# Moving DMA issues among a displaced convolution's engine queues

## The chip, the core and the metric

The kernel runs on one core of a Trainium2 chip. Its time is the device time of one execution in microseconds (us), and a comparison uses the median over several runs. The engines are PE (TensorE: matrix products, with PEld its weight loads), DVE (VectorE), ACT (ScalarE), POOL (GpSimd) and SP (SyncE). A DMA is issued by an instruction in the queue of one engine (here SP and ACT) and carried out by 16 shared DMA engines.

## The reference

Input x has shape (32, 384, 64, 64) in float32, with 48 offsets of two numbers. Each image is normalised in groups of 12 channels, each group of 8 channels is shifted by its rounded offset (zeros come in from outside), a 5 x 5 Gaussian of the offset's fraction is applied per channel, and the input is added.

```
def _gn(v, G=32, eps=1e-5):            # 12 channels a group
    g = v.reshape(B_, G, C_ // G, H_, W_)
    return ((g - mean(g)) / sqrt(var(g) + eps)).reshape(v.shape)

def _L0_conv_ref(x, offset):           # offset: (48, 2)
    off_round = round(offset)
    disp = _displace(x.reshape(B, 48, 8, h, w), off_round)
    d = field[None] + (offset - off_round)[:, None, None, :]
    kernel = exp(-sum(d * d, -1) / (2.0 * SIGMA ** 2))
    kernel = kernel / sum(kernel, axis=(1, 2))
    return depthwise_conv5x5(disp, repeat(kernel, 8))

out = x + _L0_conv_ref(_gn(x), offset)
```

## The kernel before

Shift and filter are separable, so each channel's plane is multiplied from both sides by small matrices: `ay` for the rows (the y products, line 750) and `ax` for the columns (the x products, line 762). The 384 channels are taken in 16 superblocks `c` of 24 channels, and each superblock in 16 steps `s` of two images (`B = 2`); `t` counts steps over the whole kernel. One step's input is a slot `xin[:, s]` of SBUF, 16 slots in all; the result is added in place in the slot and stored from there. A step's load is two DMAs on SP, one for each image (line 199), and its store is two DMAs on ACT (line 674). SP loads slot s for the next superblock when the slot's store has landed (`stored[s]`).

Steps are worked in rounds of four (`QUAD`), four rounds a superblock, 64 rounds in all. Each engine runs its own hand-written order and they meet through semaphores. In the order of one round on PE: the x products of its steps, `x_products(0)` to `x_products(3)`, 96 matmuls each; then y products of the next round's steps (`y_even`, `y_odd`, 96 matmuls each), with the statistics' sums (line 737, 8 matmuls) behind the first and the third. `x_products(0)` waits for `sums_ready`; `x_products(1)` waits for all four copies of the y results (`y_ready`, `last_lane_ready`); `x_products(2)` waits for copy_third of step t and DVE's addition of step t, and `x_products(3)` for those of step t+1.

ACT's round, in order, is: store 0 of the last round, `copy_y(t)` (PSUM to `y`, line 651), `normalise(t+2)` (line 640), `copy_y(t+1)`, store 1, `normalise(t+3)`, `copy_y(t+2)`, stores 2 and 3, `copy_y(t+3)`, `copy_third(t)` and `copy_third(t+1)` (line 668, PSUM to `x2`), `normalise(t+4)`, `copy_third(t+2)`, `normalise(t+5)`, `copy_third(t+3)`. What stands behind a DMA issue in this order starts once the issue is through. DVE computes the statistics of coming steps (line 502, three a step, running 17 ahead), copies one lane of y (526), reduces the sums (518) and adds two thirds of the result (533); POOL turns sums into coefficients, normalises the other half (341) and adds the last third (332).

At the start SP loads slots 0 to 11 at once and 12 to 15 behind a wait on `x_done`, which reaches 4 when `x_products(1)` of the first round is done. `y_done` counts y products, the first, third and so on only together with the sums behind them; it reaches 5 when the y product and the sums behind the first round's x products are done. At the end ACT issues the last round's four stores and then raises `norm0_ready` (line 724), for which PE's last pass, one pair of y products that no output reads, waits. SP ends when all stores have landed (line 211).

Of the kernel before, what the change touches and what calls it, by code (L numbers as in the profile page):

```python
# [11 lines left out]
P = 128  # L12
POSITIONS = 48
B = 2
# [4 lines left out]
NSUPER = CH // SUPER  # L19
# [10 lines left out]
STEPS = BATCH // B  # L30
TOTAL = NSUPER * STEPS
SLOTS = 16
PAIR = 2
QUAD = 4
# [11 lines left out]
def displaced_conv(nc: bass.Bass, x: bass.AP, offset: bass.AP, out: bass.AP):  # L46

    def tiled(a):
        return a.rearrange("(m b) (s q a) (h r) w -> m b s (a h) q (r w)", b=B, s=NSUPER, q=Q, a=LANES, r=R)

    x_t, out_t = tiled(x), tiled(out)
    off_row = offset.rearrange("(o p) k -> o (p k)", o=1)

    with ExitStack() as ctx:
        def sb(name, shape, dt=F32):
            return ctx.enter_context(nc.sbuf_tensor(name, shape, dt))

        def sem(name):
            return ctx.enter_context(nc.semaphore(name))


        xin = sb("xin", [P, SLOTS, Q, ROW])
# [69 lines left out]
        stored = [sem(f"stored{i}") for i in range(SLOTS)]  # L132
# [15 lines left out]
        y_done = sem("y_done")  # L148
# [3 lines left out]
        x_done = sem("x_done")  # L152
        x2_ready = sem("x2_ready")
        result0_ready = sem("result0_ready")
        result1_ready = sem("result1_ready")
# [20 lines left out]
        ADDS = 2  # L176
        SPARE = 2
# [3 lines left out]
        def run(one_round):  # L181

            def superblock(c, head=False, tail=False):
                for g in range(ROUNDS):
                    one_round(c, g, head and g == 0, tail and g == ROUNDS - 1)
            superblock(0, head=True)
            with nc_engine[0].Fori(1, NSUPER - 1) as c:
                superblock(c)
            superblock(NSUPER - 1, tail=True)
# [3 lines left out]
        @block.sync  # L193
        def _(sync):
            sync.dma_start(off[:, :, :], off_row.to_broadcast([P, 2 * POSITIONS])).then_inc(off_loaded, 16)

            def load(c, s):
                for b in range(B):
                    sync.dma_start(xin[b:P:B, s], x_t[s, b, c]).then_inc(loaded[s], 16)

            for s in range(SLOTS):
                if s == FIRST:

                    sync.wait_ge(x_done, ADDS * PAIR)
                load(0, s)
            with sync.Fori(1, NSUPER) as c:
                for s in range(SLOTS):
                    sync.wait_ge(stored[s], 16 * B * c)
                    load(c, s)
            for s in range(SLOTS):  # L210
                sync.wait_ge(stored[s], 16 * B * NSUPER)

# [384 lines left out]
        def _(act):  # L597
# [15 lines left out]
            def square(c, part):  # L613
                source, target = ((t_int, t_isq), (t_full, t_fsq))[part]
                act.wait_ge(dist_ready, 2 * c + part + 1)
                nc.scalar.activation(target[:], source[:], ACT.Square).then_inc(sq_ready, 1)

            def exponential(c):
                act.wait_ge(sq_ready, 2 * c + 2)
                nc.scalar.activation(t_exp[:], t_fsq[:], ACT.Exp, scale=-2.0).then_inc(exp_ready, 1)  # L620

            def fill_rows(c, k):

                act.wait_ge(made, c + 1)
                if k == 0:

                    act.wait_ge(half0_ready, STEPS * (c + 1))
                for part in range(1 - k, B):
                    filled_k = nc.scalar.activation(ay[:, k].rearrange("p r (m b) -> p (r m) b", b=B)[:, :, part],  # L629
                                                    t_msk[:, k, 0:R].rearrange("p r m -> p (r m)"), ACT.Identity,  # L630
                                                    scale=same[:, part:part + 1])
                filled_k.then_inc(mats_ready[k], STEPS)

            def normalise(t, s, quad, first=False):
                act.wait_ge(coef_ready, (s // PAIR + 1) if first else quad + 2)
                if not (first and s < 2):
                    act.wait_ge(y_done, t - 1)
                cv, col = s // QUAD % 2, GROUPS * (s % QUAD)
                cols = slice(0, QG * HW)
                nc.scalar.activation(norm[:, s % 2, :, cols].rearrange("p r (q w) -> p q r w", w=HW),  # L640
                                     xin[:, s, 0:QG].rearrange("p q (r w) -> p q r w", w=HW),
                                     ACT.Identity, bias=bias[:, cv, col:col + 1],
                                     scale=rstd[:, cv, col:col + 1]).then_inc(norm0_ready, 1)

            def copy_y(t, j, first):

                lanes = LANES if j == 2 else LANES - 1
                act.wait_ge(y_done, t + 1)
                if not first:
                    act.wait_ge(x_done, ADDS * (t - QUAD + 1))  # L650
                nc.scalar.activation(y[:, j].rearrange("p k r a m -> p a (k r) m")[:, 0:lanes],  # L651
                                     ps[:, j % 2, 0:lanes, 0:POS * P].rearrange("p a (n m) -> p a n m", m=32),
                                     ACT.Copy).then_inc(y_ready, 1)
# [10 lines left out]
            def copy_third(t, s, first=False):  # L664
                act.wait_ge(x_done, ADDS * (t + 1))
                if not first:
                    act.wait_ge(result0_ready, t - QUAD + 1)
                nc.scalar.activation(x2[:, s % QUAD], ps[:, s % 2, 2:4, 0:ROW], ACT.Copy).then_inc(x2_ready, 1)  # L668

            def store(c, s, t):  # L670
                act.wait_ge(result0_ready, t + 1)
                act.wait_ge(result1_ready, SPARE + t + 1)
                for b in range(B):
                    act.dma_start(out_t[s, b, c], xin[b:P:B, s]).then_inc(stored[s], 16)

            def one_round(c, g, first, last):
                t, s, quad = STEPS * c + QUAD * g, QUAD * g, ROUNDS * c + g
                group_follows = c is not NSUPER - 1

                def store_of_last_round(j):  # L680
                    if not first:
                        store(c if g else c - 1, (s - QUAD + j) % STEPS, t - QUAD + j)

                if group_follows:
                    if g == 1:
                        square(c + 1, 0)
                    if g == 2:
                        square(c + 1, 1)
                    if g == 3:
                        exponential(c + 1)  # L690
                store_of_last_round(0)
                copy_y(t, 0, first)
                act.wait_ge(last_lane_ready, t + 1)
                normalise(t + 2, s + 2, quad, first)
                copy_y(t + 1, 1, first)
                store_of_last_round(1)
                act.wait_ge(last_lane_ready, t + 2)
                normalise(t + 3, s + 3, quad, first)
                copy_y(t + 2, 2, first)
                store_of_last_round(2)  # L700
                store_of_last_round(3)
                copy_y(t + 3, 3, first)
                border = g == ROUNDS - 1 and group_follows
                if border:
                    fill_rows(c + 1, 0)
                copy_third(t, s, first)
                copy_third(t + 1, s + 1, first)
                if not last:
                    normalise(t + 4, (s + 4) % STEPS, quad + 1)
                copy_third(t + 2, s + 2, first)  # L710
                if border:
                    fill_rows(c + 1, 1)
                if last:
                    store(c, s, t)
                else:
                    normalise(t + 5, (s + 5) % STEPS, quad + 1)
                copy_third(t + 3, s + 3, first)
                if last:
                    for j in range(1, QUAD):
                        store(c, s + j, t + j)  # L720
            run(one_round)

            act.wait_ge(norm0_ready, TOTAL)
# [151 lines left out]
```

## Time and profile before

| | us |
|---|---|
| median of 3 runs | 1249.34 (1246.99 to 1251.42) |
| profiled execution, its own time | 1246.37 |
| its span, first to last instruction | 1244.5 |
| PE busy | 1155.9 (93%) |
| DVE busy | 968.7 (78%) |
| POOL busy | 853.0 (69%) |
| ACT busy | 750.7 (60%) |
| DMA, mean over the span | 324 GB/s, 402.99 MB |

The span is the trace's, and the execution's own time has 1.9 us more around it. Busy time of an engine leaves out the instructions that issue DMAs: ACT's 60% does not hold the time for which its queue is taken by them. In a timeline ACTq and SPq are these issues.

### The profile page before, as it was taken

The numbers are of one execution on the slowest core, as the hardware profiler recorded it, in microseconds if no ns is written. First come the engines' busy times: TensorE is split into PE (matmuls) and PEld (weight loads), VectorE is DVE, ScalarE is ACT, GpSimd is POOL, SyncE is SP. The second block draws the span as 40 slices with busy tenths as digits, with TensorE's granted clock in tenths as the row PEclk, the third lists the DMA queues.
The fourth block names the chain that finished last, engine by engine and source line by source line (L and its number), as shares of the span: only waits on it lengthen the run. The fifth ranks groups of instructions, "written<-read, shape, count | busy, mean of one in ns | idle before, by whom it ended". The sixth has DMA issues, their size and how long they took to land. (4 is left out here: it accounts for less than half of the span.)

```text
span 1244.5 us, 113105 instructions
## 1 busy us (share of the span) xinstructions
PE 1155.9 (93%) x50608; PEld 1130.8 (91%) x50608; DVE 968.7 (78%) x1373; ACT 750.7 (60%) x874; POOL 853.0 (69%) x1176
## 2 busy tenths in 40 slices
PE   7799999999999999999999999999999999999997
PEld 7799999989989999999889999999999999999997
DVE  8578878877877878878778878878778788878762
ACT  4465665655656665665666666666666666656562
POOL 7477676676776766766776766866766776766763
PEclk9899999999999999999999999999999999999998
DMA  9599999999999999999999999999999999999966
GB/s 305 182 326 332 330 344 343 326 342 329 334 337 330 330 344 329 336 341 327 335 325 321 350 343 326 343 347 325 344 334 317 349 322 347 340 345 330 343 201 202
DMA packets 409763, 402.99 MB, mean 324 GB/s; under 512 B 16528, under 2 KB 409744, under 8 KB 409744
## 3 DMA queue, kind: packets, MB, share of 16 engines
q10 hardware_dynamic: 204800, 201.36, 48.9%
q1 hardware_dynamic: 204944, 201.41, 48.9%
q8 instruction: 8, 0.13, 0.1%
q14 instruction: 11, 0.09, 0.0%
HBM read 201.38 MB, written 201.33 MB: 324 GB/s over the span
## 5 line engine op out<-in xcount | busy, mean ns | idle before, releaser
L750 PE MATMUL ps<-ay,norm 32*128 32x128 f32 x24768 | 749.4, 274 | 10.0 <-ACTq L724 6.6
L750 PEld LDWEIGHTS ps<-ay,norm 32*128 32x128 f32 x24768 | 716.9, 188 | 22.1 <-issue 8.9
L651 ACT ACTIVATE y<-ps 128x1152 f32<-128x1152 f32 (+1 forms) x256 | 310.1, 1211 | 349.5 <-PE ps L762 156.9
L502 DVE BATCH_NORM_STATS2 stats<-xin 128x6 f32<-128x512 f32 x768 | 482.5, 693 | 0.0
L762 PEld LDWEIGHTS ps<-ax,y 64*64 64x64 f32 x24576 | 379.2, 135 | 84.6 <-issue 77.0
L762 PE MATMUL ps<-ax,y 64*64 64x64 f32 x24576 | 388.3, 219 | 72.2 <-issue 69.0
L533 DVE TENSOR_TENSOR xin<-ps,xin 128x1024 f32<-128x1024 f32 x256 | 313.6, 1225 | 145.4 <-PE ps L762 145.2
L341 POOL TENSOR_SCALAR norm<-xin,rstd,bias 128x768 f32<-128x768 f32 x256 | 251.9, 987 | 126.1 <-issue 105.9
L332 POOL TENSOR_TENSOR xin<-x,xin 128x512 f32<-128x512 f32 x256 | 322.5, 1281 | 7.7 <-ACT x L668 7.5
L640 ACT ACTIVATE norm<-xin,bias,rstd 128x768 f32<-128x768 f32 x256 | 261.3, 1021 | 35.3 <-issue 34.9
L668 ACT ACTIVATE x<-ps 128x512 f32<-128x512 f32 x256 | 151.3, 591 | 86.0 <-PE ps L762 85.9
L314 POOL TENSOR_TENSOR mean_sq<-both 128x8 f32<-128x8 f32 (+1 forms) x65 | 50.9, 784 | 207.9 <-DVE both L518 205.9
L526 DVE COPY y<-ps 128x384 f32<-128x384 f32 x192 | 106.2, 553 | 65.1 <-PE ps L737 40.6
L324 POOL TENSOR_TENSOR rstd<-var,mhalf 128x8 f32<-128x8 f32 (+1 forms) x65 | 105.8, 1627 | 5.1
L518 DVE TENSOR_REDUCE both<-ps 128x24 f32<-128x288 f32 x63 | 28.8, 458 | 48.1 <-ACT y L651 48.1
L737 PE MATMUL ps<-summands,ones 32*128 32x72 f32 (+1 forms) x1040 | 47.8, 250 | 1.0 <-POOL summands L295 1.0
L737 PEld LDWEIGHTS ps<-summands,ones 32*128 32x128 f32 x1040 | 42.9, 190 | 1.5 <-issue 0.9
L629 ACT ACTIVATE ay<-t_msk,same 128x256 f32<-128x256 f32 x48 | 23.4, 525 | 2.4 <-DVE ay L495 2.4
L295 POOL TENSOR_TENSOR summands<-stats 128x24 f32<-128x24 f32 (+1 forms) x65 | 15.0, 230 | 9.8 <-POOL summands L293 9.7
L487 DVE SCALAR_TENSOR_TENSOR t_msk<-t_isq,t_exp 128x960 f32<-128x960 f32 x16 | 18.4, 1149 | 0.0
L321 POOL TENSOR_TENSOR var<-spread,mean_sq 128x8 f32<-128x8 f32 (+1 forms) x65 | 14.0, 215 | 5.2 <-POOL spread L319 0.2
L319 POOL TENSOR_TENSOR spread<-inner,both 128x8 f32<-128x8 f32 (+1 forms) x65 | 13.8, 213 | 5.4
(63 smaller groups left out, 215.2 us busy)
## 6 DMA issues: line engine op xcount, KB each, us to landing
xin<-in_x_dram SPq DMA_DIRECT2D x512, 384.0 KB, 5.8
out_dram<-xin ACTq DMA_DIRECT2D x512, 384.0 KB, 5.1
off<-in_L_conv_offset_dram SPq DMA_DIRECT2D x1, 48.0 KB, 3.6
```

Source lines behind the costliest of these rows:

```text
L324: pool.tensor_tensor(rstd[:, v, part], var[:, v, part], mhalf[:, part], ALU.pow).then_inc(small, 1)
L332: pool.tensor_tensor(at, x2[:, s % QUAD], at, ALU.add).then_inc(result0_ready, 1)
L341: pool.tensor_scalar(norm[:, s % 2, :, cols].rearrange("p r (q w) -> p q r w", w=HW), xin[:, s, QG:].rearrange("p q (r w) -> p q r w", w=H ...
L502: nc.vector.bn_stats(stats[:, s // QUAD % 2, s % QUAD, n, :], xin[:, s].rearrange("p (g q) f -> p q f g", g=GROUPS)[:, n]).then_inc(bn_don ...
L526: nc.vector.tensor_copy(y[:, j].rearrange("p k r a m -> p a (k r) m")[:, LANES - 1], ps[:, j % 2, LANES - 1, 0:POS * P].rearrange("p (n m) ...
L533: nc.vector.tensor_tensor(at, ps[:, s % 2, 0:2].rearrange("p h (k f) -> p h k f", k=2), at, ALU.add).then_inc(result1_ready, 1)
L640: nc.scalar.activation(norm[:, s % 2, :, cols].rearrange("p r (q w) -> p q r w", w=HW), xin[:, s, 0:QG].rearrange("p q (r w) -> p q r w", ...
L651: nc.scalar.activation(y[:, j].rearrange("p k r a m -> p a (k r) m")[:, 0:lanes], ps[:, j % 2, 0:lanes, 0:POS * P].rearrange("p a (n m) -> ...
L668: nc.scalar.activation(x2[:, s % QUAD], ps[:, s % 2, 2:4, 0:ROW], ACT.Copy).then_inc(x2_ready, 1)
L737: last = nc.tensor.matmul(ps[:, v, a, place], ones[rows, :], summands[rows, part].rearrange("p t n s -> p (t n s)"), start=True, stop=True)
L750: last = nc.tensor.matmul(ps[:, v, a, P * k:P * (k + 1)], norm[rows, v, r, P * k:P * (k + 1)], ay[rows, k, r, :], start=(r == 0), stop=(r ...
L762: last = nc.tensor.matmul(ps[outs, v, 2 * (k // 2) + h, at:at + HW], y[rows, j, k, r].rearrange("p a m -> p (a m)")[:, outs], ax[rows, k], ...
```

## The change

Four edits. SP's loads of slots 12 to 15 in the first superblock wait for `y_done` 5 instead of `x_done` 4. In each round ACT issues store 1 behind `normalise(t+3)` instead of ahead of it, and store 3 behind `copy_y(t+3)` instead of ahead of it. In the last round ACT issues each store's first image alone, and SP issues the second image, waiting for the same two semaphores.

```diff
--- before.py
+++ after.py
@@ -201,12 +201,17 @@
             for s in range(SLOTS):
                 if s == FIRST:
 
-                    sync.wait_ge(x_done, ADDS * PAIR)
+                    sync.wait_ge(y_done, QUAD + 1)
                 load(0, s)
             with sync.Fori(1, NSUPER) as c:
                 for s in range(SLOTS):
                     sync.wait_ge(stored[s], 16 * B * c)
                     load(c, s)
+
+            for s in range(STEPS - QUAD, STEPS):
+                sync.wait_ge(result0_ready, TOTAL - STEPS + s + 1)
+                sync.wait_ge(result1_ready, SPARE + TOTAL - STEPS + s + 1)
+                sync.dma_start(out_t[s, 1, NSUPER - 1], xin[1:P:B, s]).then_inc(stored[s], 16)
             for s in range(SLOTS):
                 sync.wait_ge(stored[s], 16 * B * NSUPER)
 
@@ -667,10 +672,10 @@
                     act.wait_ge(result0_ready, t - QUAD + 1)
                 nc.scalar.activation(x2[:, s % QUAD], ps[:, s % 2, 2:4, 0:ROW], ACT.Copy).then_inc(x2_ready, 1)
 
-            def store(c, s, t):
+            def store(c, s, t, images=B):
                 act.wait_ge(result0_ready, t + 1)
                 act.wait_ge(result1_ready, SPARE + t + 1)
-                for b in range(B):
+                for b in range(images):
                     act.dma_start(out_t[s, b, c], xin[b:P:B, s]).then_inc(stored[s], 16)
 
             def one_round(c, g, first, last):
@@ -693,13 +698,13 @@
                 act.wait_ge(last_lane_ready, t + 1)
                 normalise(t + 2, s + 2, quad, first)
                 copy_y(t + 1, 1, first)
-                store_of_last_round(1)
                 act.wait_ge(last_lane_ready, t + 2)
                 normalise(t + 3, s + 3, quad, first)
+                store_of_last_round(1)
                 copy_y(t + 2, 2, first)
                 store_of_last_round(2)
+                copy_y(t + 3, 3, first)
                 store_of_last_round(3)
-                copy_y(t + 3, 3, first)
                 border = g == ROUNDS - 1 and group_follows
                 if border:
                     fill_rows(c + 1, 0)
@@ -711,13 +716,13 @@
                 if border:
                     fill_rows(c + 1, 1)
                 if last:
-                    store(c, s, t)
+                    store(c, s, t, images=1)
                 else:
                     normalise(t + 5, (s + 5) % STEPS, quad + 1)
                 copy_third(t + 3, s + 3, first)
                 if last:
                     for j in range(1, QUAD):
-                        store(c, s + j, t + j)
+                        store(c, s + j, t + j, images=1)
             run(one_round)
 
             act.wait_ge(norm0_ready, TOTAL)
```

## Rows read from the trace of the kernel before

**Rows 1.** The page: DMA queue, costliest groups (busy, mean ns, idle before), issues with us to landing
```profile
q8 instruction: 8, 0.13, 0.1%
...
L502 DVE BATCH_NORM_STATS2 stats<-xin 128x6 f32<-128x512 f32 x768 | 482.5, 693 | 0.0
...
xin<-in_x_dram SPq DMA_DIRECT2D x512, 384.0 KB, 5.8
out_dram<-xin ACTq DMA_DIRECT2D x512, 384.0 KB, 5.1
```

**Rows 2.** Windows: us; busy of PE, PEld, DVE, ACT, POOL; clock; DMA share, GB/s
```profile
64.10:1188.76 1124.66, 1059.03 (x47041) 1036.41 (x47040) 901.23 (x1259) 698.17 (x809) 788.65 (x1068) 1.00 1.01 335
...
798.00:812.00 14.00, 13.91 (x633) 13.61 (x629) 12.65 (x18) 9.85 (x13) 11.05 (x12) 1.00 1.09 379
```

**Rows 3.** Waits of PE from 64.10 to 1188.76: us in total, times, longest
```profile
PE ps L762 <- issue: 61.4, 76, 1.7
```

**Rows 4.** Timeline of a round in mid-kernel: start, us, engine, line, operation [idle before <-releaser]
```profile
602.61 1.13 ACT L651 ACTIVATE y<-ps 128x1152 f32<-128x1152 f32 x1 [0.68 <-PE ps L750]
...
602.80 1.39 ACTq L674 DMA_DIRECT2D out_dram<-xin  x2
603.26 3.12 DVE L502 BATCH_NORM_STATS2 stats<-xin 128x6 f32<-128x512 f32 x5
...
604.32 1.03 ACT L640 ACTIVATE norm<-xin,bias,rstd 128x768 f32<-128x768 f32 x1 [0.57 <-issue]
...
605.39 2.96 PE L750 MATMUL ps<-ay,norm 32*128 32x128 f32 x96
...
605.66 4.74 ACTq L674 DMA_DIRECT2D out_dram<-xin  x4
...
608.45 1.63 PE L762 MATMUL ps<-ax,y 64*64 64x64 f32 x96
...
610.57 1.13 ACT L651 ACTIVATE y<-ps 128x1152 f32<-128x1152 f32 x1 [3.64 <-PE ps L762]
...
611.59 0.59 ACT L668 ACTIVATE x<-ps 128x512 f32<-128x512 f32 x1
...
611.79 4.42 PE L762 MATMUL ps<-ax,y 64*64 64x64 f32 x287 [1.72 <-issue]
```

**Rows 5.** Timeline of the rounds behind the last load
```profile
1188.76 1.63 PE L762 MATMUL ps<-ax,y 64*64 64x64 f32 x96
...
1190.60 4.43 PE L762 MATMUL ps<-ax,y 64*64 64x64 f32 x288 [0.21 <-issue]
...
1203.81 3.12 ACTq L674 DMA_DIRECT2D out_dram<-xin  x4
...
1206.42 1.63 PE L762 MATMUL ps<-ax,y 64*64 64x64 f32 x96
```

**Rows 6.** Timeline of the start
```profile
40.36 16.90 SPq L199 DMA_DIRECT2D xin<-in_x_dram  x10
...
42.63 2.10 PE L762 MATMUL ps<-ax,y 64*64 64x64 f32 x128 [1.40 <-issue]
...
49.02 0.47 PE L762 MATMUL ps<-ax,y 64*64 64x64 f32 x2 [4.30 <-issue]
...
49.42 5.50 PE L750 MATMUL ps<-ay,norm 32*128 32x128 f32 x96
```

**Rows 7.** Windows of 1 us at the start and the end, columns as before
```profile
49.00:50.00 1.00, 0.98 (x10) 0.86 (x14) 0.00 (x0) 0.47 (x1) 0.00 (x0) 0.50 1.08 374
...
1239.00:1240.00 1.00, 1.00 (x32) 1.00 (x28) 0.00 (x0) 0.00 (x0) 0.00 (x0) 0.58 0.58 197
```

**Rows 8.** Timeline of the end
```profile
1230.55 6.21 ACTq L674 DMA_DIRECT2D out_dram<-xin  x6
1231.14 1.26 POOL L332 TENSOR_TENSOR xin<-x,xin 128x512 f32<-128x512 f32 x1 [0.18 <-ACT x L668]
...
1236.96 4.30 PE L750 MATMUL ps<-ay,norm 32*128 32x128 f32 x96 [6.60 <-ACTq L724]
```

## The prediction

> **What bounds the kernel now.** I read the page first. Every slot's transfer is paired: 512 loads issued by SP, 512 stores issued by ACT, 384 KB each, landing some 5.8 and 5.1 us after issue; the statistics on DVE have 0.0 us of idle time before them, so no load is late now [rows 1]. Then the windows. Between the first round with stores and the last round with loads lie 1124.66 us with 47041 matmuls. A round has 784 (384 y products, 384 x products, 16 sums), so that is 60 rounds of 18.74 us [rows 2]. Then the waits of PE in that stretch: one kind only, 61.4 us in 76 times before an x product, "issue" by name, 1.02 us a round [rows 3]. The timeline of one round shows whose it is. x_products(0) starts at 608.45 and lasts 1.63, but the next x products start only at 611.79, behind a gap of 1.72. They need all four y copies, and ACT starts the last, copy_y(t+3), at 610.57, though its y product was done at about 608.4. Between copy_y(t+2) and it stand the issues of stores 2 and 3: four DMAs from 605.66 for 4.74 us, to 610.40 [rows 4]. So ACT's queue of instructions, by the time that DMA issues hold it, sets PE's gap. The rounds behind the last load confirm it from the other side: there the four issues take 3.12 us, the gap is 0.21, and a round from 1188.76 to 1206.42 takes 17.66; without the gap it would be 17.45 [rows 5]. That is the floor that PE gives.
>
> **A law from these rows.** Call F the duration of those four issues. The round at 608.45 has F = 4.74 and gap 1.72, the late round F = 3.12 and gap 0.21: the gap is about F - 3.0 in the one and F - 2.9 in the other [rows 4, 5]. The mean gap of 1.02 then stands for a mean F of about 4.0.
>
> **Store 3 behind copy_y(t+3), store 1 behind normalise(t+3).** No instruction is added or removed in the middle. Copy_y(t+3) now waits for two fewer issues. At a mean of 1.19 each (4.74 / 4) they cost 2.4 us; without them it can start at 608.5, ends at 609.6, inside x_products(0) and well ahead of 610.1, and the gap before x_products(1) is nothing. The cost: normalise(t+3) goes ahead of store 1's issue. It starts when copy_y(t+1) ends, at 602.61 + 1.13 = 603.74, and store 1's two issues start some 0.9 us later than at 602.80, say by 0.85 [rows 4]. They still end by 605.1, before the sums and y product at 605.39 let copy_y(t+2) go, so that copy keeps its time. Queued behind store 3 are now copy_third(t), copy_third(t+1), normalise(t+4). What is late next is copy_third(t): x_products(2) needs it, and x_products(2) could start 2 x 1.63 = 3.26 after 608.45. Its start is at 605.66 + 0.85 + F + 0.17, its end 0.60 later, so x_products(2) waits
>
> 605.66 + 0.85 + F + 0.17 + 0.60 + 0.05 - 611.71 = F - 4.38 us.
>
> With F = 4.0 that is nothing, with 4.74 it is 0.36. F will not stay: the same 16 DMAs (6.29 MB) move in a shorter round, so stores meet loads more often. The rates say how far it can go. The stage moves 335 GB/s at a DMA share of 1.01; 14 us in it ran at 379 and 1.09 [rows 2]. A round of 17.8 us needs 353, which the engines can give, but with only 7% of spare time instead of 12%. Bounds: F = 3.12 (no loads beside) gives 17.45 a round; F with each store at half of 379 GB/s, 2.07 us, four of them 8.3, gives 21. The steady rounds are the nearest rows by far, so I take F = 4.7, a wait of 0.35, and a round of 17.80. Gain: 60 x (18.74 - 17.80) = 56.4 us. The two late rounds give 2 x 0.21 = 0.4.
>
> Store 1 is the tightest for the loads. Now its second issue ends at 604.19, it lands at 609.3, the load goes out by 610.5 and lands at 616.3; the statistics that read it are the fourth of the five begun at 603.26, one round later: 605.1 + 18.8 = 623.9. That is 7.6 us early [rows 1, 4]. Afterwards the store is 0.85 later and the round 0.94 shorter: 5.8 us early, which hides the move. If that cover goes, DVE waits and the round is what the transfers allow.
>
> **Loads 12 to 15 held until y_done 5.** They now go out from 40.36. x products pause for 1.40 us ahead of 42.63, but for 4.30 us ahead of 49.02, under the loads, and then PE runs at half clock: the y product at 49.42 takes 5.50 for what takes 2.96 at 605.39 [rows 4, 6]; the granted clock was 0.50 of full, which is 1.2 of 2.4 GHz, after that idle stretch [rows 7]. The pauses fit the instruction queue's 8 packets of 0.13 MB together, some 16 KB each [rows 1], queued behind load packets. With the loads held until the y product of step 4 is through (49.42 - 2.9 + 2.8, about 49.3 on the new clock), the pause should be like its neighbour's: 4.30 - 1.40 = 2.9 saved. No half clock: 2.5 on the first y product and 0.5 on the next, 3.0. Against it: the refills that fall under the loads now may cost up to the same 2.9, and slot 12 is wanted by DVE at about 53 (behind two lane copies and four statistics of 0.69), some 4 us after its issue where landings take 5.8, up to 1.8, partly covered by DVE's waits for ACT. Between 1.2 and 5.9, I take 4.0. The Trainium skill (Runtime: NRT & Kernel Launch, Instruction fetch mechanics) says that instructions are refilled in 16 KiB blocks and that crossing one is mostly hidden. By that rule the start term would be nothing and the sum 1186; the 4.30 us pause beside one of 1.40 speaks against it.
>
> **The last round's stores by two engines.** Now ACT issues six DMAs from 1230.55 for 6.21 us, and the last PE pass (which no output reads) waits 6.60 us for ACT to be through, starts at 1236.96 and ends the span [rows 8]. With one DMA a store on ACT, its last issue waits for POOL's last addition at 1231.14 + 1.26 = 1232.4 and ends at about 1233.1. The pass starts 3.8 us earlier, still partly at half clock, as now. SP is free by then. The last bytes left at 1239.6 [rows 7]; SP is not held by ACT's copy_third(t+2) and (t+3), two of 0.6 us as in [rows 4], so they leave at 1238.5 or so, and SP's wait ends near the new end of PE, 1240.4. Between 2.0 and 4.6, I take 3.5. The Trainium skill (DMA: Bandwidth & Descriptors, Issuing engines are not separate DMA queues) says that a second issuer saves only the sequencer's issue time. By that rule the bytes still end at 1239.6, and with the 2 us that the same page gives for a completion the term would be 2.6, an estimate, and the sum 1183.
>
> **Sum.** 56.4 + 0.4 + 4.0 + 3.5 = 64.3. The profiled execution took 1246.37 (span 1244.5, 1.9 around it): 1182.1. The median of the runs shown is 3.0 above that execution; I say 1184.
>
> **Rivals.**
> Half of it comes back at x_products(2): F grows to 5.2, wait 0.8, round 18.25. 60 x 0.49 = 29.4, with the ends 37.3: 1209. For it: F already varies with load traffic (3.12 to 4.74). Against: it needs a quarter more than the mean F.
> The transfers bind: the round stays at 18.74 because the queue stays as badly filled as now (335 of 379 GB/s), the 5.8 us of lead is used up, and statistics wait for loads. Only the ends gain, 7.9: 1238. Against it: idle stretches of the queue come from having nothing queued, and a backlog fills them.
> Slower: copy_third(t) behind store 3. If the four issues average 1.55 us, halfway from 1.19 to 2.07, F = 6.2, the wait is 1.8, the round 19.27: 60 x 0.53 = 31.8 lost, 7.9 gained, 1270. It decides from F = 5.8 on. Against it: no steady row shows more than 4.74.
> The change does nothing measurable: F near 5.8, about 1246.
>
> **How the numbers follow.** A measurement of this kernel can tell about 0.3%, 3.7 us. Main case 0.59 (own range 1160 to 1198: rounds of 17.45 to 18.05), half 0.21, transfers bind 0.07, nothing 0.05, slower 0.08. The first three are faster: 0.87. The range goes from 1163, where the round is near the floor and the ends give their most, to 1222, a round of 18.45; that leaves out 0.2.
>
> **What would show it.** Right: PE's gap behind x_products(0) gone, ACT's copy_y(t+3) starting 0.1 us behind the y product, four issues in two pairs around it, rounds of 17.8, 350 GB/s or more in mid-kernel, no pause of 4 us and no half clock near 49, the last PE pass starting near its release at 1233 on the old clock less the gain. Wrong: a gap before x_products(2) with ACT's queue as cause (the law F - 4.38 failed in F), DVE's statistics waiting for a load (the lead), or a long pause of PE moved to about 52 (the start term).

## The result and the profile after

| | before | changed |
|---|---|---|
| median of 3 runs, us | 1249.34 | 1189.17 (1188.73 to 1189.46) |
| ratio, 95% interval | | 0.9519 (0.9491 to 0.9546) |
| profiled execution, its own time / span | 1246.37 / 1244.5 | 1188.73 / 1186.6 |

The forecast was 1184, 1163 to 1222. Between the two profiled spans lie 57.9 us. The first x product of each round cuts them into four parts:

| part | before | changed | less | forecast |
|---|---|---|---|---|
| start, to x_products(0) of round 2 | 64.1 | 62.3 | 1.8 | 4.0 |
| 60 rounds | 18.74 each | 17.85 each | 53.4 | 56.4 |
| two rounds behind the last load | 17.66 each | 17.22 each | 0.9 | 0.4 |
| end, from the last x_products(0) | 20.4 | 18.6 | 1.8 | 3.5 |

Lines of the changed kernel lie 5 higher than before (762 is now 767). The page of the changed kernel, in the groups that [rows 1] show of before:

```profile
L507 DVE BATCH_NORM_STATS2 stats<-xin 128x6 f32<-128x512 f32 x768 | 482.8, 694 | 3.7 <-DMA xin<-in_x_dram 3.5
...
xin<-in_x_dram SPq DMA_DIRECT2D x512, 384.0 KB, 6.1
out_dram<-xin ACTq DMA_DIRECT2D x508, 384.0 KB, 6.6
out_dram<-xin SPq DMA_DIRECT2D x4, 384.0 KB, 3.9
```

Stores land 1.5 us later than before (6.6 against 5.1), loads 0.3. The statistics waited 3.5 us for loads, all of it near the start, as the timeline below shows. The window from round 2 to round 62 of the changed kernel, columns as in [rows 2]:

```profile
62.33:1133.57 1071.24, 1046.00 (x47040) 1029.32 (x47040) 899.70 (x1259) 699.01 (x808) 787.25 (x1068) 1.00 1.05 353
```

1071.24 us are 60 rounds of 17.85, and the stage moves 353 GB/s at a DMA share of 1.05, against 335 and 1.01. PE's waits in this stretch (us in total, times, longest):

```profile
PE ps L767 <- ACT x L673: 16.3, 33, 1.5
PE ps L767 <- DVE xin L538: 5.3, 6, 0.9
PE ps L767 <- DVE both L523: 2.4, 1, 2.4
PE ps L767 <- issue: 0.5, 2, 0.3
```

The 2.4 us are the wait just ahead of the first of these rounds and belong to the start. Inside the 60 rounds, 61.4 us before x products with cause "issue" [rows 3] have become 22.1, of which 16.3 are waits for copy_third on ACT. (Taken between the starts of matmuls, small gaps included, the x products' gaps are 1.18 us a round before and 0.56 now.) The timeline of the changed kernel shows one of the long ones, in the last round of a superblock:

```profile
381.00 1.89 ACTq L679 DMA_DIRECT2D out_dram<-xin  x2
...
383.48 3.03 PE L767 MATMUL ps<-ax,y 64*64 64x64 f32 x192
383.53 1.13 ACT L656 ACTIVATE y<-ps 128x1152 f32<-128x1152 f32 x1 [1.28 <-PE ps L755]
383.72 2.92 ACTq L679 DMA_DIRECT2D out_dram<-xin  x2
...
386.89 0.53 ACT L634 ACTIVATE ay<-t_msk,same 128x256 f32<-128x256 f32 x1 [2.22 <-DVE xin L538]
...
387.31 1.05 ACT L673 ACTIVATE x<-ps 128x512 f32<-128x512 f32 x2
...
388.02 3.03 PE L767 MATMUL ps<-ax,y 64*64 64x64 f32 x192 [1.51 <-ACT x L673]
```

copy_y(t+3) starts 0.05 us behind x_products(0), where in [rows 4] it started 2.1 behind, and x_products(0) and (1) run through without a gap (192 matmuls in 3.03). Then ACT's queue is held by store 3 from 383.72 to 386.64. One copy into `ay` that only such a border round has (386.89) stands ahead of copy_third(t), and x_products(2) starts at 388.02, 1.51 late. The rounds behind the last load, in the same kernel:

```profile
1133.57 5.83 PE L767 MATMUL ps<-ax,y 64*64 64x64 f32 x384
...
1150.79 5.83 PE L767 MATMUL ps<-ax,y 64*64 64x64 f32 x384
```

17.22 from one to the next, 0.44 less than in [rows 5], and all of it lies in the x products. Without a gap 384 of them take 5.83 us and the last 288 take 4.43 [rows 5], so x_products(1) starts 1.40 behind x_products(0); in [rows 5] it started 1190.60 - 1188.76 = 1.84 behind. The gap that is printed as 0.21 cost 0.44. The 1.63 us of an x_products(0) that stands alone run to the end of its last matmul, and in an unbroken row the next block starts before that end.

The start of the changed kernel, beside [rows 6]:

```profile
43.35 2.10 PE L767 MATMUL ps<-ax,y 64*64 64x64 f32 x128 [1.68 <-issue]
...
47.27 0.32 PE L767 MATMUL ps<-ax,y 64*64 64x64 f32 x2 [1.83 <-issue]
...
47.66 2.96 PE L755 MATMUL ps<-ay,norm 32*128 32x128 f32 x96
...
50.85 24.49 SPq L199 DMA_DIRECT2D xin<-in_x_dram  x16
...
56.89 1.91 DVE L507 BATCH_NORM_STATS2 stats<-xin 128x6 f32<-128x512 f32 x3 [1.96 <-DMA xin<-in_x_dram]
...
60.36 1.30 DVE L507 BATCH_NORM_STATS2 stats<-xin 128x6 f32<-128x512 f32 x2 [1.56 <-DMA xin<-in_x_dram]
...
62.33 5.83 PE L767 MATMUL ps<-ax,y 64*64 64x64 f32 x384 [2.42 <-DVE both L523]
```

The pause ahead of the last two x products is 1.83 us where it was 4.30, and the y product behind it takes 2.96 where it took 5.50. Of these 5.0 us most is given back: the two pauses ahead of it are 0.5 us longer together than before, the loads go out at 50.85, statistics wait ahead of 56.89 (1.96) and 60.36 (1.56), the sums behind them are late, and x_products(0) waits 2.42 for them. A single trace is weak evidence here, because the start scatters from one execution to the next. Over the traces of all kernels of this document, x_products(0) of round 2 starts at 62.5 to 66.1 in the five with the early loads and at 59.6 to 64.3 in the seven with the loads held until y_done 5; the means, 64.0 and 62.2, are 1.8 apart as well. The end, beside [rows 8]:

```profile
1170.38 5.45 POOL L337 TENSOR_TENSOR xin<-x,xin 128x512 f32<-128x512 f32 x4 [6.75 <-ACT x L673]
...
1171.68 4.78 SPq L214 DMA_DIRECT2D out_dram<-xin  x4
...
1173.96 3.40 ACTq L679 DMA_DIRECT2D out_dram<-xin  x3
...
1177.56 5.50 PE L755 MATMUL ps<-ay,norm 32*128 32x128 f32 x96 [3.71 <-ACTq L729]
```

ACT's last three issues take 3.40 us and end at 1177.36, 9.35 behind the last x_products(0); before, the last six ended at 1236.76, 12.7 behind it. But the last PE pass takes 9.0 us where it took 7.2. Windows of the same stretch:

```profile
1176.00:1178.00 2.00, 0.45 (x8) 0.48 (x12) 0.00 (x0) 0.00 (x0) 0.00 (x0) 0.71 1.04 347
1178.00:1180.00 2.00, 2.00 (x44) 2.00 (x44) 0.00 (x0) 0.00 (x0) 0.00 (x0) 0.50 1.05 345
```

The granted clock was at its lower level (1.2 of 2.4 GHz) when the pass began, and stayed there for its first 5.5 us; before, it was low at the start of the pass too, but back at full by the end of the first product. About half of the earlier start was lost so in this trace. The end scatters as well: from the last x_products(0) on it takes 20.4 to 21.5 us in the five traces whose last round is not split and 15.6 to 18.6 in the nine with the split. The means are 21.0 and 16.8, 4.2 apart.

### The profile page after: what moved, and what is told of

Read it like the earlier page. It is cut to its first block and busy times, and to the rows that moved or that the text cites. A ratio compares the mean times of both kernels' runs of the same rounds, so it can differ in the third digit from the quotient of the medians.

```text
span 1186.6 us, 113109 instructions
## 1 busy us (share of the span) xinstructions
PE 1142.1 (96%) x50608; PEld 1123.1 (95%) x50608; DVE 966.9 (81%) x1373; ACT 752.5 (63%) x874; POOL 851.0 (72%) x1176
## 5 line engine op out<-in xcount | busy, mean ns | idle before, releaser
L767 PE MATMUL ps<-ax,y 64*64 64x64 f32 x24576 | 386.1, 219 | 32.7 <-ACT x L673 16.3
L673 ACT ACTIVATE x<-ps 128x512 f32<-128x512 f32 x256 | 148.4, 591 | 98.1 <-PE ps L767 81.8
L531 DVE COPY y<-ps 128x384 f32<-128x384 f32 x192 | 106.0, 552 | 57.9 <-PE ps L742 35.5
L492 DVE SCALAR_TENSOR_TENSOR t_msk<-t_isq,t_exp 128x960 f32<-128x960 f32 x16 | 18.4, 1149 | 0.0
L833 PE MATMUL ps<-idle 32*128 32x56 f32 x224 | 12.5, 416 | 5.1 <-ACT idle L605 5.1
```

Of the source, the lines that this page charges most:

```text
L531: nc.vector.tensor_copy(y[:, j].rearrange("p k r a m -> p a (k r) m")[:, LANES - 1], ps[:, j % 2, LANES - 1, 0:POS * P].rearrange("p (n m) ...
L767: last = nc.tensor.matmul(ps[outs, v, 2 * (k // 2) + h, at:at + HW], y[rows, j, k, r].rearrange("p a m -> p (a m)")[:, outs], ax[rows, k], ...
```

## The experiments

Theory A is that of the prediction: ACT's queue, held by DMA issues, sets PE's gaps, and the two ends give the rest. Theory B gives the ends a larger part, theory C lets the transfers set the round. Each ratio is to the kernel before in the same set of runs, and the row "the change" is a second set of five runs of the changed kernel. The table has the mean round from the traces (60 rounds from the second on, from one x_products(0) to that 60 rounds later) and the mean end of the last issue of store 3, behind the start of x_products(0), over the 54 rounds from the seventh on.

| kernel | us, median | ratio to before, interval | round, us | store 3 issued by |
|---|---|---|---|---|
| before | 1249 to 1251 | | 18.74 | +1.19 |
| the change | 1188.6 | 0.9520 (0.9498 to 0.9542) | 17.85 | +2.35 |
| both store moves alone | 1191.6 | 0.9525 (0.9495 to 0.9554) | 17.88 | +2.42 |
| store 3 alone | 1186.2 | 0.9493 (0.9465 to 0.9521) | 17.75 | +1.78 |
| store 1 alone | 1285.6 | 1.0273 (1.0239 to 1.0307) | 19.40 | +1.94 |
| change, store 3 behind copy_third(t) | 1162.3 | 0.9303 (0.9275 to 0.9331) | 17.49 | +3.26 |
| held loads alone | 1247.2 | 0.9982 (0.9966 to 0.9998) | | |
| split last round alone | 1246.3 | 0.9971 (0.9958 to 0.9985) | | |
| change, loads released by x_done 8 | 1188.1 | 0.9506 (0.9490 to 0.9521) | | |
| change, loads a sixth | 1167.9, one run | | 17.51 | +1.70 |
| change, store 1 back | 1184.1 | 0.9488 (0.9472 to 0.9504) | 17.76 | +1.76 |
| store 3 behind copy_third(t), store 1 back | 1179.1 | 0.9446 (0.9433 to 0.9459) | 17.68 | +3.27 |
| three edits together | 1171.3 | 0.9384 (0.9368 to 0.9399) | 17.59 | +3.36 |

**Both store moves alone.** The middle part of the diff on the kernel before.

> The kernel before with the two store moves alone (stores 1 and 3), first loads and last round as before. Theory A, the order of ACT's queue sets the gain: PE's round falls from 18.74 to 17.85 us and the two late rounds to 17.2, so 54 us less, about 1195. Theory B, a good part of the gain comes from the held loads and the split last round: over 1205. Theory C, the transfers set the round: the stores' order does nothing beyond noise, 1249.

1191.6, 0.9525: theory A. The ends add nothing that stands clear of the intervals here; theory C is out.

**Store 3 alone.**

```diff
-                store_of_last_round(3)
                 copy_y(t + 3, 3, first)
+                store_of_last_round(3)
```

> The kernel before with store 3 alone moved behind copy_y(t+3); store 1 stays ahead of normalise(t+3). Theory A: the gap before x_products(1) goes as in the full change. Store 1 keeps its earlier start, so the wait at x_products(2), 0.63 us a round in the changed kernel, is nearly nothing, while PE's floor stays at the 17.45 of the rounds behind the last load: rounds of 17.5 to 17.6, 1176 to 1182, faster than both moves together. Rival: the six issues end when the transfers let them, whatever their start, so the 0.63 stays and the floor is 0.23 worse: rounds of 18.1, about 1210.

1186.2. This one edit gives all of the gain. PE's waits in its 60 rounds, same columns:

```profile
PE ps L762 <- issue: 5.6, 25, 0.3
PE ps L762 <- ACT x L668: 3.1, 8, 0.6
```

The wait for copy_third falls from 16.3 to 3.1 us, because store 3 is through at +1.78 instead of +2.35: the start of store 1 does carry through to the sixth issue. The round is 17.75 and not the 17.5 to 17.6 I had expected: three rounds of four take 17.6, the border round 18.2. The place of store 1 shows in the part of the round behind the x products (y products and sums): it takes 11.84 us on average here and 11.80 in the kernel before, against 11.52 with both moves. But the rounds behind the last load take 17.22 here too, with store 1 in its old place:

```profile
1128.02 5.83 PE L762 MATMUL ps<-ax,y 64*64 64x64 f32 x384
...
1145.24 5.83 PE L762 MATMUL ps<-ax,y 64*64 64x64 f32 x384
```

**Store 1 alone.**

```diff
                 copy_y(t + 1, 1, first)
-                store_of_last_round(1)
                 act.wait_ge(last_lane_ready, t + 2)
                 normalise(t + 3, s + 3, quad, first)
+                store_of_last_round(1)
```

> The kernel before with store 1 alone moved behind normalise(t+3); store 3 stays ahead of copy_y(t+3). Theory A: the four issues ahead of copy_y(t+3) end 0.85 us later while PE's floor falls by 0.23, so the gap before x_products(1) grows from 1.0 to about 1.9 and the round from 18.74 to 19.3: about 1285. Rival, the issues end when the transfers let them: gap as before, round 18.5, about 1236.

1285.6, slower by 2.7%, as theory A said (1285). The timeline shows the four issues together ahead of copy_y(t+3), ending later against PE's work:

```profile
603.57 4.66 ACTq L674 DMA_DIRECT2D out_dram<-xin  x4
...
606.05 1.64 PE L762 MATMUL ps<-ax,y 64*64 64x64 f32 x96
...
608.39 1.13 ACT L651 ACTIVATE y<-ps 128x1152 f32<-128x1152 f32 x1 [3.56 <-PE ps L762]
...
609.62 4.45 PE L762 MATMUL ps<-ax,y 64*64 64x64 f32 x288 [1.93 <-issue]
```

They end at 608.23, 2.2 behind x_products(0), and the gap is 1.93; the mean end over the rounds is +1.94 where before it was +1.19.

**Store 3 behind copy_third(t).** On the changed kernel:

```diff
                 copy_y(t + 3, 3, first)
-                store_of_last_round(3)
...
                 copy_third(t, s, first)
+                store_of_last_round(3)
                 copy_third(t + 1, s + 1, first)
```

> The changed kernel with store 3 put one step further back, behind copy_third(t) instead of ahead of it. Theory A, the wait at x_products(2) is ACT's queue: it goes, copy_third(t+1) is then next and wanted some 1.4 us later; rounds of 17.25 to 17.4, about 1156 to 1162. Rival, the transfers are at their limit (353 GB/s in the stage): 17.3 would want 364 GB/s and they don't give it; the wait turns up elsewhere, at a load or a later copy, and the time stays within 0.3% of 1189.

1162.3, 0.9303, the fastest of all kernels here, 2.3% below the changed kernel (0.9303 against 0.9520). A window in mid-kernel and one round's timeline:

```profile
300.00:1000.00 700.00, 693.24 (x31395) 686.12 (x31392) 601.37 (x842) 467.65 (x541) 525.23 (x711) 1.00 1.06 360
```

```profile
304.22 1.13 ACT L656 ACTIVATE y<-ps 128x1152 f32<-128x1152 f32 x1 [1.28 <-PE ps L755]
304.26 5.83 PE L767 MATMUL ps<-ax,y 64*64 64x64 f32 x384
...
305.94 0.60 ACT L673 ACTIVATE x<-ps 128x512 f32<-128x512 f32 x1
306.13 1.39 ACTq L679 DMA_DIRECT2D out_dram<-xin  x2
...
307.68 0.60 ACT L673 ACTIVATE x<-ps 128x512 f32<-128x512 f32 x1 [1.14 <-PE ps L767]
```

360 GB/s, so 353 was not the transfers' limit. All 384 x products run in 5.83 us without a gap, with store 3's two issues (1.39 us) between two copies that both come in time. For the x products, copy_third(t) was the last thing whose wait mattered. What is left is the border round, 17.93 against 17.34 for the others. Of PE's waits in the 60 rounds 3.5 us in 14 times are for normalise(t+2), ahead of the third y product of a border round. ACT does it late because it stands behind store 0 and copy_y(t), and store 0 waits for POOL's last addition:

```profile
313.96 1.13 ACT L656 ACTIVATE y<-ps 128x1152 f32<-128x1152 f32 x1 [2.07 <-POOL xin L337]
314.99 1.02 ACT L645 ACTIVATE norm<-xin,bias,rstd 128x768 f32<-128x768 f32 x1
...
316.15 2.96 PE L755 MATMUL ps<-ay,norm 32*128 32x128 f32 x96 [0.27 <-ACT norm L645]
```

**Loads a sixth of their size.** On the changed kernel:

```diff
                     sync.wait_ge(stored[s], 16 * B * c)
-                    load(c, s)
+                    for b in range(B):
+                        sync.dma_start(xin[b:P:B, s, 0:1], x_t[s, b, c, :, 0:1]).then_inc(loaded[s], 16)
```

> The changed kernel with each load of the superblocks after the first cut to the first of six channel rows (one sixth of the bytes); the rest of a slot is stale, so the output is not the reference's. It shows what the loads' traffic does to ACT's issues. Theory A, stores wait in their queue because loads share the engines: the four issues fall from about 4.7 to 2.6 us, the wait at x_products(2) goes and the round is the floor of 17.2, 1151. Rival, an issue costs what it costs by itself: the wait stays, 1185.

```profile
300.00:1000.00 700.00, 697.08 (x31362) 686.63 (x31360) 600.54 (x840) 466.90 (x540) 525.91 (x710) 1.00 0.65 210
```

At 210 GB/s store 3 is through at +1.70 instead of +2.35 and the wait at x_products(2) is nearly gone (0.11 us a round left in the x products, between starts as the 0.56 above). So the loads' traffic does lengthen the issues: without most of it, the sixth is through 0.65 us sooner. The time was 1167.9 and not 1151: the floor of 17.22 was reached only in rounds behind the last load. Here too three rounds of four take 17.3 and the border round 18.0, and that was missing from my sum.

**The ends, each alone.** Held loads:

```diff
-                    sync.wait_ge(x_done, ADDS * PAIR)
+                    sync.wait_ge(y_done, QUAD + 1)
```

> The kernel before with the loads of slots 12 to 15 held until y_done 5, nothing else. Theory A, from the changed kernel's trace, where the first round with stores begins 1.8 us sooner: the pause of 4.3 us and the half clock go (5.9 us), but statistics wait for slots 12 and 13 and give 3.5 to 4 back: 1.5 to 2.5 us less than before, 1247. Rival, my forecast's term: 4.0 less, 1245.5. Rival, the later loads cost more than the pause: 1249 or more.

2.6 us less (0.2 to 4.2 by the interval): A and my forecast's 4.0 both lie in it. The trace has the shorter pause, 1.56, but with it a y product that is again slow, and x_products(0) of round 2 starts at 64.34, no sooner than the 64.10 of before. The y product and its window:

```profile
46.60 0.32 PE L762 MATMUL ps<-ax,y 64*64 64x64 f32 x2 [1.56 <-issue]
...
46.99 4.59 PE L750 MATMUL ps<-ay,norm 32*128 32x128 f32 x96
```

```profile
49.00:51.00 2.00, 2.00 (x47) 2.00 (x44) 0.00 (x0) 0.00 (x0) 0.00 (x0) 0.51 0.87 298
```

The split last round, SP's second images and `images=1` on ACT:

> The kernel before with the last round's stores split between ACT and SP, nothing else. Theory A, from the changed kernel's trace: PE's last pass is released 3.3 us sooner, but more of it runs at half clock, so 1.8 us less, 1247.5. Rival, my forecast's term: 3.5 less, 1246. Rival: the stores' landing sets the end and nothing is gained.

3.5 us less (1.9 to 5.2). Its last pass starts 9.8 behind the last x_products(0), where before it was 12.9, and its first product takes as long as in [rows 8]:

```profile
1233.48 4.29 PE L755 MATMUL ps<-ay,norm 32*128 32x128 f32 x96 [3.51 <-ACTq L729]
```

The end took 2.8 less in this trace and 1.8 in the changed kernel's; given the scatter of single traces, the 3.5 of the runs is the better number.

**Earlier release of the loads.** On the changed kernel:

```diff
-                    sync.wait_ge(y_done, QUAD + 1)
+                    sync.wait_ge(x_done, ADDS * QUAD)
```

> The changed kernel with the loads of slots 12 to 15 released by x_done 8 (x products of the first round done) instead of y_done 5, some 3.2 us sooner. Theory A, statistics wait for late slots: both waits go, the first round's sums come 2.4 us sooner, 1187. Rival: PE's next refill of instructions, at about 48, falls under the loads and the pause comes back: 1189 or more.

1188.1 against 1189.2 and 1188.6: not to be told apart. Its trace has statistics waiting 0.28 and 0.42 us instead of 1.96 and 1.56, and x_products(0) of round 2 at 58.7 instead of 62.3, and the only other trace with this release (the three edits together) has 60.1. With y_done 5 the seven traces have 59.6 to 64.3, so an earlier start is likely, but not shown; in the time, the scatter of 60 rounds hides it.

**Store 1 back in its place.** First with store 3 behind copy_y(t+3), beside the changed kernel itself:

> The changed kernel with store 1 put back ahead of normalise(t+3), store 3 stays behind copy_y(t+3), held loads and split last round stay. Beside it in the same call the changed kernel itself. Theory A: 0.85 us earlier at x_products(2) takes most of the wait there, 0.23 is lost to the floor; by the single traces of the store moves (17.75 against 17.88 a round) 7 us less than the changed kernel, 1182. Rival: the two cancel, within 3 us.

> The changed kernel once more, for the comparison with the three beside it on one chip: 1189.

1184.1 against 1188.6. The first pair of kernels (store 3 alone, both moves) had the same sign, 1186.2 against 1191.6. Each time the intervals of the ratios overlap a little; the mean rounds, 17.76 against 17.86 and 17.75 against 17.88, say the same. Then with store 3 behind copy_third(t):

> The changed kernel with store 3 behind copy_third(t), and store 1 put back ahead of normalise(t+3). Theory A: with the wait at x_products(2) gone, the start of store 1 no longer matters there, and what is left of it is the floor, which is 0.23 to 0.44 us a round higher because y_odd waits for normalise(t+3): 1162 + 14 to 26, 1176 to 1188. Rival, an earlier store 1 also gives the four issues time that they still lack: 1162 or less.

1179.1 against 1162.3, 0.9446 against 0.9303, intervals apart. So the same move, store 1 behind normalise(t+3), costs some 5 us in the one order and gives some 17 in the other. The two traces differ by 14.2 us: 11.5 in the 60 rounds (17.68 against 17.49), the rest in the start and the end, which the move is not known to touch.

**Three edits together.** On the changed kernel, store 3 behind copy_third(t), the release by x_done 8, and:

```diff
-                store_of_last_round(0)
                 copy_y(t, 0, first)
                 act.wait_ge(last_lane_ready, t + 1)
                 normalise(t + 2, s + 2, quad, first)
+                store_of_last_round(0)
                 copy_y(t + 1, 1, first)
```

> The changed kernel with store 3 behind copy_third(t) and two edits more: store 0 behind normalise(t+2) instead of ahead of copy_y(t), and the first loads released by x_done 8. In the trace with store 3 behind copy_third(t), three rounds of four take 17.35 and every fourth 17.93, where ACT waits for POOL's last third ahead of store 0 and copy_y(t) with it. Theory A: that wait no longer holds the copies, all rounds 17.25 to 17.35, 8 to 10 us less, and 1 to 3 from the first loads: 1150 to 1153. Rival, the transfers set what is left (365 GB/s wanted): 1159 or more.

A miss: 1171.3, slower than without the move of store 0. The border round stayed at 17.91 (17.93 without the move of store 0), and the others went from 17.34 to 17.49. The wait ahead of the third y product, shown above, is gone, but another took its place: on average over the 15 border rounds the sums behind the third y product start 0.23 late, and the last y product 0.15 more. So ACT's wait for POOL was a cause of the longer round in the one order, and its removal laid the next wait bare. Stores 0, 1 and 2 now come close together, and the timeline shows copy_y(t+3) held again, from about 305.9 to 306.44:

```profile
303.42 2.85 ACTq L679 DMA_DIRECT2D out_dram<-xin  x2
...
305.90 6.20 PE L767 MATMUL ps<-ax,y 64*64 64x64 f32 x384
...
306.44 1.13 ACT L656 ACTIVATE y<-ps 128x1152 f32<-128x1152 f32 x1 [1.75 <-PE ps L755]
```

What the sums of the border round wait for in this order stays open: four of the waits are for POOL's part of them, 0.8 us in all, and POOL, ACT and DVE all have more work in such a round. With store 3 behind copy_third(t) and store 1 back, the border round is only 0.06 longer than the others (17.72 against 17.66).

## Why the prediction was right

**What bounds the kernel.** Right, and shown: moving only the issues of store 3 gives 5.1%, moving only those of store 1 costs 2.7%, with no other instruction changed.

**The law.** Its form held (issues end late, the next copy is late, PE waits), and the next place was the right one, x_products(2) behind copy_third(t). A gap before x_products(2) with ACT's queue as its cause was named as a sign that F had grown. The gap is there, but F had not grown: the four issues of stores 2 and 3 take 3.4 us on average, each counted by itself, in both kernels. Three other terms were wrong.

- When x_products(2) could start: I took 2 x 1.63 = 3.26 behind x_products(0). In an unbroken row the blocks start 1.41 apart, so it is 2.82. This is the term that failed most: by F - 4.38 an end at +2.35 would give no wait at all, and in 51 of the 60 rounds there is one.
- When store 3 is through: 605.66 + 0.85 + 4.7 - 608.45 = +2.76, measured +2.35. I had added 0.85 although the same paragraph lets copy_y(t+2), and with it store 2, keep its time. In fact store 3's first issue starts at +0.21, behind the start of copy_y(t+3), and its two issues take 0.65 and 1.32 on average.
- What stands between: 0.17 + 0.60 + 0.05, measured 0.17 + 0.60 + 0.14. In border rounds the `ay` copy of 0.53 comes on top, which I had left out.

With the measured terms the wait is 2.35 + 0.91 - 2.82 = 0.44 and some 0.5 more in every fourth round, 0.56 on average. The trace has 0.54 at x_products(2), 0.40 in ordinary rounds and 0.96 in border rounds, where I had 0.35. That a wait can't be less than nothing adds little, since only 9 rounds of 60 had none.

**The floor.** I had 17.45, and it was 17.22. The step is the same: a gap was taken at its printed length, 0.21, where it cost 0.44. It was no gain of the change, for store 3 alone has late rounds of 17.22 too. What store 1's place does change, beside the loads, is the part of the round behind the x products. In four pairs of kernels that differ in it, this part is shorter with store 1 behind normalise(t+3): 11.51 against 11.80 us, 11.52 against 11.84 twice, and 11.72 against 11.87 with store 3 behind copy_third(t). About half of that lies between the start of the second sums and that of the y product behind them (0.34 before, 0.18 in the changed kernel), so y_odd's wait for normalise(t+3) is the likely cause; it is not shown by itself. So the sum 17.45 + 0.35 stands against a measured 17.22 + 0.56 + 0.07, and that 17.80 and 17.85 agree so well is in part luck.

**Store 1's move.** I costed it at 0.85 us of delay that F = 4.0 would cover. It is a loss here, by 4.5 and 5.4 us in two pairs of kernels whose intervals overlap a little. In the traces of the first pair it gives 0.32 us a round behind the x products and costs 0.45 in them. It pays only once copy_third(t) is out of store 3's way.

**The loads' lead of 5.8 us.** Enough: outside the start no statistics waited.

**The start term**, 4.0, measured 1.8 in the trace, 1.8 between the means of the traces and 2.6 (0.2 to 4.2) in the runs of the held loads alone. The two gains that I named came in this trace (2.5 and 2.5), but the second, no half clock, came in only four of the nine traces with held loads. The loss from slot 12 was put at up to 1.8 and was 2.4 at x_products(0), through slots 12 and 13. Instruction refills are not hidden here. In the trace of before one packet of the instruction queue falls into the window from 40 to 42 and one into that from 44 to 46, so each pause has its own. PE paused 1.83 us at 45 with no load in flight (1.6 to 2.1 in the nine traces with held loads), and 4.30 under the loads (3.5 to 5.4 in five). The Trainium skill (Runtime: NRT & Kernel Launch, Instruction fetch mechanics) calls them mostly hidden; for this first pass through PE's code the measurement decides against it.

**The end term**, 3.5, measured 1.8 in the trace of the change, 3.5 in the runs of the split alone and 4.2 between the means of the traces. The release came 3.3 us sooner where I had 3.8; in the trace of the change the clock took half of it back. The transfers end 14.3 us behind the last x_products(0) with the split alone, where before it was 15.5; I had 1.1 sooner. The Trainium skill (DMA: Bandwidth & Descriptors, Issuing engines are not separate DMA queues) holds as far as it goes: the issuer's time is what was saved, and here PE waited for just that.

**The rivals.** That the transfers bind is excluded: 360 GB/s and 0.9303 with a better order. Half the gain lost at x_products(2) happened in border rounds only (18.4 on average, the others 17.7). The slower case needed four issues of 5.8 us or more; from the start of store 2 to the end of store 3 it is 4.9 on average in the changed kernel, with copy_y(t+3) between, and 5.6 at most. (Its mean of 1.55 is not halfway from 1.19 to 2.07; that would be 1.63 and a still slower case.)

## What to carry to other kernels

A DMA issue costs its engine's queue time, and behind other issues beside busy transfers more of it; an engine that is busy 60% can still set the round. Look at what stands behind each issue and how soon another engine wants it, and put the issue behind the last thing that is wanted soon, one place further than looks necessary. The value of one such move depends on the others: measure them apart. Take how soon a block of work could start from the starts in a row without a gap, not from the printed length of a block that stands alone. And do not size a term of a few microseconds from one trace when the start and end scatter by as much.

## What the runs showed of the hardware

A store's issue took 0.62 us when few had gone just ahead of it, even beside full loads: both issues of store 3 did so on average where it stood behind copy_third(t), at 360 GB/s. In the changed kernel the second issue of store 3, the last of six in a row broken only by two copies, took 1.32 us on average, and 0.71 with small loads. So the number of issues just ahead and the traffic of the other queue both count.

Half clock did not need a long pause, and two executions of one kernel differ in it. With the held loads alone, PE paused 1.56 us at 46.60, yet the granted clock was 0.51 in the window from 49 to 51 and the y product took 4.59 us. In the trace above the changed kernel paused 1.83 us at the same place and kept full clock, but its second trace has the low level again, behind a pause of 1.56:

```profile
45.33 0.32 PE L767 MATMUL ps<-ax,y 64*64 64x64 f32 x2 [1.56 <-issue]
45.72 4.59 PE L755 MATMUL ps<-ay,norm 32*128 32x128 f32 x96
```

```profile
47.00:49.00 2.00, 2.00 (x46) 2.00 (x42) 0.00 (x0) 0.18 (x1) 0.00 (x0) 0.50 0.92 308
```

All five traces with the early loads went to half clock there, and five of the nine with held loads. No run here says what makes the difference.
